# Edge-block steps of a graph layer: the bias of Q is added by VectorE as it copies Q out of PSUM

## The chip, the cores and the metric

The kernel runs on one core of one Trainium2 chip. The metric is the device time of one execution in microseconds. Five engines run programs of their own and meet at semaphores: TensorE (PE; its weight loads are listed as PEld), VectorE (DVE), ScalarE (ACT), GpSimd (POOL) and SyncE (SP), which issues most of the DMAs.

## The reference, cut to what matters

There are 50,000 nodes of 256 features and 12,500 edges. The first layer is an attention over the edges, with 8 heads of 32:

```python
qkv = x @ W_qkv.T + b_qkv
Q, K, V = ...                                   # 256 columns each
att = einsum('mhd,mhd->mh', Q[receivers], K[senders]) / sqrt(32)
attention = softmax of att over the edges that share a receiver
out = segment_sum(attention[:, :, None] * V[senders], receivers)
x = layernorm(x + out @ W_ff.T + b_ff)
```

A second layer (embeddings of the senders, filters from the edge attributes, a segment sum, one more product and a layernorm) follows. All of it is float32, and the output is 50,000 x 256.

## The kernel before, in words

Nodes without an edge need only the two layernorms and one product. So a first pass goes over all nodes as if none had an edge, and a last pass works out the rows that are receivers again and scatters them over the first result.

The first pass has 98 steps (`for g in range(G)` on every engine), each with 512 nodes: four groups of 128 rows. Nine steps in (`LEAD = 9`) the 49 edge blocks join in: step g also works on block b = g - 9, with 256 edges. These 49 steps, 9 to 57, are the edge-block steps. In a block the rows of x for the receivers (`xd`) and the senders (`xs`) were gathered by GpSimd two steps ahead. The order within a step is written out by hand, engine by engine:

- **PE**: `columns(b)` transposes xd and xs into PSUM banks A and A+1 (8 passes); `z_product(g, 0)` is the first half of the node product (12 passes, lines 845 to 847); `x_transposes(g + 1)` (8 passes, line 831); then `q_product(b)` into bank C, `k_product(b)` into bank A, `v_product(b)` into bank A+1 (14, 14 and 12 passes) and `z_product(g, 1)` (12 passes). Q and K are products in three parts (high x high, high x low, low x high), accumulated in PSUM, and each half of them starts with one pass that puts the bias row there (line 888). `q_product` waits for `xd_hi` and `xd_lo`, and `k_product` for `xs_hi` and `xs_lo`, before their first passes.
- **ScalarE**: `parts(b)` copies the transposed rows out of PSUM (`xd_hi`, `xdT`, `xs_hi`), then squares, the copy `z_hi`, a scaling (`final`), and at the end of the step `q_copy(b)` (line 1156) and `v_copy(b)` (line 1163).
- **VectorE**: `y(g - 1, 1)` (line 1442), `stats(g + 2)` (line 1414), `receiver_low(b)` (`xd_lo`, line 1468), `y(g, 0)`, `source_low(b)` (`xs_lo`, line 1473), `moments`, two small reciprocals, `z_low(g + 1)` (line 1479), `scores(b)` (lines 1487 and 1492) and its quarter of `final(g - 1)` (line 1460).
- **GpSimd**: `z_add(g + 3)` (line 682), four gathers of rows (lines 730 and 736), and one or two gathers of types (line 724), two in every other step.

`scores(b)` multiplies K, which it reads from bank A, by Q, which it reads from `qr` in SBUF, and adds up each head. `columns(b + 1)` on PE waits for that product (`e_prod`), since it writes into bank A again, and `q_product(b + 1)` waits until bank C was read (`e_q`).

Of the kernel before, what the change touches and what calls it, by code (L numbers as in the profile page):

```python
# [31 lines left out]
P = 128  # L32
ALU = mybir.AluOpType
ACT = mybir.ActivationFunctionType
# [12 lines left out]
def after(eng, sem, count):  # L47

    if count > 0:
        eng.wait_ge(sem, count)  # L50


def build(nc, x, src, dst, attr, weight, ntype, w_qkv, b_qkv, w_ff, b_ff, table, w_dist, b_dist, w_comb, b_comb, out):
    N, D = x.shape
# [34 lines left out]
    def sb(name, shape, dt=F32):  # L89
        return ctx.enter_context(nc.sbuf_tensor(name, shape, dt))  # L90

    def sem(name):
        return ctx.enter_context(nc.semaphore(name))
# [4 lines left out]
    ps = ctx.enter_context(nc.psum_tensor("ps", [P, 8, 512], F32))  # L98

    def bank(k):  # L100
        return ps[:, k, :].rearrange("p (c n) -> p c n", c=2)
# [42 lines left out]
    w_hi, w_lo = (sb(n, [P, DC, 3 * D], F32R) for n in ("w_hi", "w_lo"))  # L144
    b_raw = sb("b_raw", [P, 3, D])
    b_hi = sb("b_hi", [P, 3, D], F32R)
    b_rows = sb("b_rows", [P, 3, D], F32R)
    ones_r = sb("ones_r", [P, P], F32R)
# [82 lines left out]
    xs_hi, xs_lo, xd_hi, xd_lo = (sb(n, [P, 2, EB], F32R) for n in ("xs_hi", "xs_lo", "xd_hi", "xd_lo"))  # L231
    ze_hi, ze_lo = (z_lo[:, 0, c, :].rearrange("p (c n) -> p c n", c=2) for c in range(DC))
    xdT, vT = (sb(n, [P, 2, 2, EB]) for n in ("xdT", "vT"))
    qr, kr = (sb(n, [P, 2, EB]) for n in ("qr", "kr"))
# [84 lines left out]
    e_qp = sem("q_product")  # L319
    e_kp = sem("k_product")  # L320
    e_vp = sem("v_product")
    e_q = sem("q_copied")
    e_v = sem("v_ready")
    e_prod = sem("qk_ready")
    e_att = sem("scores_ready")
# [78 lines left out]
    def inside(g):  # L404

        return 0 <= g < G
# [9 lines left out]
    def relaxed(g):  # L416

        return g < LEAD or g >= AFTER
# [5 lines left out]
    def within(b):  # L424

        return 0 <= b < B
# [9 lines left out]
    def flat(a):  # L436
        return a.rearrange("p c n -> p (c n)")
# [6 lines left out]
    A, AB, C = 5, slice(5, 7), 7  # L444
# [373 lines left out]
    def _(pe):  # L818
        mm = pe.matmul
# [61 lines left out]
                    last = pe.transpose(bank(A + 1)[:, c, t * P:(t + 1) * P], xs[:, par, t, c * P:(c + 1) * P], ident[:])  # L881
            last.then_inc(e_xsp, 1)

        def edge_product(to, hi, lo, o):

            for t in range(2):
                e = t * P
                mm(to[:, t, :], ones_r[:], b_rows[:, o // D, :], start=True, stop=False)  # L888
                for k in range(DC):
                    mm(to[:, t, :], hi[:, k, e:e + P], w_hi[:, k, o:o + D], start=False, stop=False)  # L890
                    mm(to[:, t, :], hi[:, k, e:e + P], w_lo[:, k, o:o + D], start=False, stop=False)  # L891
                    last = mm(to[:, t, :], lo[:, k, e:e + P], w_hi[:, k, o:o + D], start=False, stop=k == DC - 1)  # L892
            return last

        def q_product(b):
            pe.wait_ge(e_xdh, b + 1)
            pe.wait_ge(e_xdl, b + 1)
            after(pe, e_q, b)
            edge_product(bank(C), xd_hi, xd_lo, 0).then_inc(e_qp, 1)

        def k_product(b):
            pe.wait_ge(e_xsh, b + 1)
            pe.wait_ge(e_xsl, b + 1)
            pe.wait_ge(e_xdc, b + 1)
            edge_product(bank(A), xs_hi, xs_lo, D).then_inc(e_kp, 1)

        def v_product(b):
            to = bank(A + 1)
# [116 lines left out]
        for g in range(G):  # L1025
            b = g - LEAD
# [59 lines left out]
    def _(act):  # L1086
        def zT_copy(g):
            for c in range(DC):
                act.wait_ge(n_tp, 2 * g + c + 1)
                after(act, n_y, 2 * (g - 1))  # L1090
                to = z_hi if in_parts(g) else zT
                act.activation(to[:, g % 2, c, :], ps[:, c, :], ACT.Identity, bias=bff_col[:, c:c + 1]).then_inc(n_tc, 1)  # L1092

        def std1(g):
            q = g % SLOTS
            np_, nj = size(g)
            act.wait_ge(n_mv, g + 1)
            after(act, n_r1, g - SLOTS + 1)
            act.activation(sd1[0:np_, q, 0:nj], mv[0:np_, q, 0:nj, 1], ACT.Sqrt, bias=eps_col[0:np_, :]).then_inc(n_s1, 1)
# [50 lines left out]
            after(act, e_vp, n)  # L1150
            act.activation(flat(xs_hi), ps[:, A + 1, :], ACT.Copy).then_inc(e_xsh, 1)

        def q_copy(b):
            act.wait_ge(e_qp, b + 1)
            after(act, e_prod, b)
            act.activation(flat(qr), ps[:, C, :], ACT.Copy).then_inc(e_q, 1)

        def v_copy(b):
            par = b % 2
            act.wait_ge(e_vp, b + 1)  # L1160
            after(act, e_vo[par], 16 * (b // 2))
            for c in range(2):
                act.activation(vT[:, par, c, :], bank(A + 1)[:, c, :], ACT.Identity, bias=bqkv[:, 4 + c:5 + c]).then_inc(e_v, 1)  # L1163
# [57 lines left out]
        for g in range(G):  # L1221
            b = g - LEAD
            if inside(g + 1):
                std1(g + 1)
            if within(b):
                parts(b)
            if inside(g - 1):
                squares(g - 1, 0)
            if relaxed(g) and inside(g + 1):
                zT_copy(g + 1)  # L1230
            if g == 4:
                act.wait_ge(s_echain, 7)
                act.activation(ct[:, 3, :], ct[:, 2, :], ACT.Sin, bias=half_pi[:], scale=-float(np.pi) / CUTOFF).then_inc(s_sin, 1)
            if inside(g - 1):
                squares(g - 1, 1)
                std2(g - 1)
            if not relaxed(g):
                zT_copy(g + 1)
            if inside(g - 2):
                final(g - 2)  # L1240
            if g == 5:
                bias_copies()
            if g == 6 or g == 7:
                weight_copies(g - 6)
            if g == 3:
                act.wait_ge(s_wready, 2)
                for k in range(DC):
                    act.activation(mix_hi[:, k, :], w_mix[:, k, :], ACT.Copy).then_inc(s_mix, 1)
            if within(b):
                q_copy(b)  # L1250
                v_copy(b)
            if g == AFTER + 13:
                act.wait_ge(c_step, step["difference"])
                act.activation(ex_c[:], run_c[:], ACT.Exp, scale=SCALE).then_inc(c_ex, 1)
            if g == AFTER + 33:
                act.wait_ge(s_tyt, 1)
                act.activation(ty_rows[:], ps[0:T, A, 0:P], ACT.Copy).then_inc(s_tyc, 1)
# [29 lines left out]
    def _(dve):  # L1287
# [193 lines left out]

        by_chunk = att[:].rearrange("p (g r h) -> p r g h", g=TL, h=H8)

        def scores(b):
            dve.wait_ge(e_kp, b + 1)
            dve.wait_ge(e_q, b + 1)
            dve.tensor_tensor(prod[:], ps[:, A, :], flat(qr), ALU.mult).then_inc(e_prod, 1)
            dve.wait_ge(e_prod, b + 1)
            heads = prod[:].rearrange("p (t h f) -> p t h f", t=2, f=HD)
            r, g = divmod(2 * b, TL)  # L1490
            if g + 1 < TL:
                dve.tensor_reduce(by_chunk[:, r, g:g + 2, :], heads, AX.X, ALU.add).then_inc(e_att, 1)
            else:
                dve.tensor_reduce(by_chunk[:, r, g, :], heads[:, 0], AX.X, ALU.add)
                dve.tensor_reduce(by_chunk[:, r + 1, 0, :], heads[:, 1], AX.X, ALU.add).then_inc(e_att, 1)
# [189 lines left out]
        for g in range(G):  # L1685
            b = g - LEAD
            if inside(g - 1):
                y(g - 1, 1)
            if inside(g - 2) and relaxed(g - 1):
                rstd2(g - 2)  # L1690
            if inside(g + 2):
                stats(g + 2)
            if within(b):
                receiver_low(b)
            y(g, 0)
            if within(b):
                source_low(b)
            if inside(g + 2):
                moments(g + 2)
            if inside(g + 1):  # L1700
                rstd1(g + 1)
            if inside(g - 1) and not relaxed(g):
                rstd2(g - 1)
            if in_parts(g + 1):
                z_low(g + 1)
            if within(b):
                scores(b)
            if inside(g - 1) and not relaxed(g):
                if relaxed(g - 1):
                    dve.wait_ge(n_od, g - 1)  # L1710
                final(g - 1)
            if g == 2:
                edge_floats()
            if g == 3:
                edge_cutoffs()
            if g == 5:
                edge_indices()
            if g == 6 or g == 7:
                weight_low(g - 6)
            if g == 7:  # L1720
                bias_parts()
            if g == 4:
                dve.wait_ge(s_mix, 2)
                for k in range(DC):
                    dve.tensor_tensor(mix_lo[:, k, :], w_mix[:, k, :], mix_hi[:, k, :], ALU.subtract).then_inc(s_mix, 1)
            if g == LEAD + 30:
                table_parts()
            softmax_step(g - AFTER)
# [44 lines left out]
```

## Time and profile before

| | |
|---|---|
| median of 3 runs | 1124.53 us (1122.92 to 1125.94) |
| profiled execution | 1127.21 us, span of its instructions 1125.5 us |
| PE busy in the span | 1058.2 us (94%) |
| VectorE busy | 918.4 us (82%) |
| ScalarE busy | 802.3 us (71%) |
| GpSimd busy | 811.4 us (72%) |
| granted TensorE clock, mean | 0.978 of full speed |
| edge-block steps | about 71 to 539 us of the span |

Busy times of the profile are sums of the durations of instructions. Matmuls are pipelined: the profile gives one of them 0.28 us while the next starts 0.12 us after it, so what a pass costs is read from the distance of two starts and not from its duration. The same holds, by less, for VectorE, where one instruction can start some hundredths before the recorded end of the one before.

### The profile page before, as it was taken

The page shows a single profiled execution, that of the slowest core. Times are in us where ns is not written, and L with a number is a line of the kernel's source. Part 1 is how long each engine was busy: PE and PEld are TensorE (multiplying, and loading weights), DVE is VectorE, ACT ScalarE, POOL GpSimd, SP SyncE. Part 2 cuts the span into 40 slices and gives each one's busy share as a digit, 9 for nine tenths or more (in the row PEclk, how much of TensorE's full clock was granted, in tenths as well). Part 3 has the DMA queues.
Part 4 walks back from the last instruction along what each step waited for, and adds up shares of the span by engine and source line. Part 5 has one row for each costly group of instructions (what it writes and reads, how often), then busy time and mean ns, then how long its engine had stood idle before and what let it go on. Part 6 is the DMA issues. An engine that isn't in the chain of part 4 may idle for free.

```text
span 1125.5 us, 25645 instructions
## 1 busy us (share of the span) xinstructions
PE 1058.2 (94%) x7302; PEld 983.2 (87%) x7302; DVE 918.4 (82%) x2643; ACT 802.3 (71%) x2452; POOL 811.4 (72%) x656
## 2 busy tenths in 40 slices
PE   5889999999999999999979799989999999999993
PEld 4679999999999999999858588879989888889882
DVE  5867888888888888888998889758888888888882
ACT  3876777777777777777767688875666666666663
POOL 5588878787888788886788888844666666666663
PEclk9999999999999999999989899989999999999997
DMA  4866666666666666665545457765666666666640
GB/s 152 305 241 215 229 228 229 224 231 221 228 217 230 208 232 216 231 219 207 190 166 200 158 206 238 276 195 164 177 174 186 188 183 186 186 189 193 186 140 33
DMA packets 121388, 227.26 MB, mean 202 GB/s; under 512 B 33588, under 2 KB 61487, under 8 KB 121185
## 3 DMA queue, kind: packets, MB, share of 16 engines
q1 hardware_dynamic: 104000, 189.54, 50.6%
q0 software_dynamic: 17248, 36.08, 11.3%
q8 instruction: 60, 0.98, 0.4%
q14 instruction: 80, 0.65, 0.2%
HBM read 137.84 MB, written 93.59 MB: 206 GB/s over the span
## 4 chain that ended last, share of the span: by engine, by line
PE 52%; DVE 26%; issue 10%; ACT 7%; SPq 2%; DVEq 1%; DMA 1%; POOL 0%; ACTq 0%; POOLq 0%
PE ps L852 7%; DVE num L1619 5%; PE ps L831 5%; PE ps L891 4%; PE ps L890 4%; PE ps L892 4%; PE ps L847 4%; PE ps L845 4%; PE ps L846 4%; DVE zeT L1630 3%; DVE est L1656 3%; DVE agg L1643 3%; PE ps L888 2%; ACT t L1196 2%; DVE msg L1639 2%
## 5 line engine op out<-in xcount | busy, mean ns | idle before, releaser
L682 POOL TENSOR_TENSOR zin<-xin,bff_row 128x1024 f32<-128x1024 f32 x98 | 233.1, 2379 | 39.3 <-DVE stat L1414 18.5
L1442 DVE SCALAR_TENSOR_TENSOR yn<-ps,r,bc 128x256 f32<-128x256 f32 x391 | 169.0, 473 | 64.0 <-PE ps L847 40.5
L852 PE MATMUL ps<-w_mix,zT 128*128 128x256 f32 x780 | 189.4, 394 | 10.1 <-ACT zT L1092 5.4
L852 PEld LDWEIGHTS ps<-w_mix,zT 128*128 128x128 f32 x780 | 147.8, 197 | 34.4 <-ACT zT L1092 10.7
L1107 ACT ACTIVATE junk<-yn 128x256 f32<-128x256 f32 x391 | 157.8, 415 | 12.3 <-DVE yn L1442 12.0
L743 POOL TENSOR_TENSOR ev<-abc,v 128x512 f32<-128x512 f32 x49 | 62.0, 1266 | 115.5 <-DVE zeT L1630 115.5
L1414 DVE BATCH_NORM_STATS2 stat<-zin 128x6 f32<-128x256 f32 x391 | 135.3, 407 | 1.9 <-issue 1.5
L724 POOL DMA_INDIRECT ty<-in_node_type_dram,src_i x98 | 103.2, 1053 | 25.7 <-issue 23.1
L730 POOL DMA_INDIRECT xd<-in_x_dram,idx x98 | 94.8, 967 | 36.1 <-PE ps L876 13.8
L755 POOL DMA_INDIRECT out_dram<-oe,idx x98 | 101.1, 1032 | 25.4 <-issue 20.2
L845 PE MATMUL ps<-mix_hi,z_hi 128*128 128x256 f32 x392 | 114.0, 291 | 2.8 <-DVE z_lo L1479 2.8
L736 POOL DMA_INDIRECT xs<-in_x_dram,idx x98 | 93.5, 954 | 29.6 <-issue 29.3
L831 PE MATMUL ps<-ident,xin 128*128 128x128 f32 (+1 forms) x782 | 103.4, 276 | 9.3 <-DMA xin<-in_x_dram 9.3
L847 PE MATMUL ps<-mix_hi,z_lo 128*128 128x256 f32 x392 | 109.9, 280 | 0.0
L846 PE MATMUL ps<-mix_lo,z_hi 128*128 128x256 f32 x392 | 109.9, 280 | 0.0
L831 PEld LDWEIGHTS ps<-ident,xin 128*128 128x128 f32 (+1 forms) x782 | 91.8, 143 | 14.7 <-issue 9.6
L1124 ACT ACTIVATE on<-yn,r 128x256 f32<-128x256 f32 (+1 forms) x229 | 101.0, 498 | 0.2 <-DVE r L1452 0.2
L973 PE MATMUL ps<-wc,agg 128*128 128x256 f32 x392 | 98.3, 379 | 0.0
L955 PE MATMUL ps<-num,wff 128*128 128x256 f32 x392 | 93.7, 382 | 0.0
L1092 ACT ACTIVATE zT<-ps,bff_col 128x512 f32<-128x512 f32 x98 | 61.8, 678 | 37.8 <-PE ps L831 37.6
L1214 ACT ACTIVATE oe<-ye,er 128x256 f32<-128x256 f32 x98 | 44.5, 501 | 61.5 <-DVE er L1679 61.5
L1163 ACT ACTIVATE vT<-ps,bqkv 128x256 f32<-128x256 f32 x98 | 41.1, 473 | 64.9 <-PE ps L914 64.9
(212 smaller groups left out, 3377.0 us busy)
## 6 DMA issues: line engine op xcount, KB each, us to landing
xin<-in_x_dram SPq DMA_DIRECT2D x97, 512.0 KB, 4.4
out_dram<-on SPq DMA_DIRECT2D x97, 512.0 KB, 2.9
xd_o<-xdT SPq DMA_DIRECT2D x49, 256.0 KB
v_o<-vT SPq DMA_DIRECT2D x49, 256.0 KB, 2.0
v<-v_o SPq DMA_DIRECT2D x49, 256.0 KB
xd<-xd_o SPq DMA_DIRECT2D x49, 256.0 KB, 4.2
abc<-a_o SPq DMA_DIRECT2D x196, 64.0 KB
sbc<-same_o SPq DMA_DIRECT2D x49, 128.0 KB, 3.8
```

Of the source, the lines that this page charges most:

```text
L682: pool.tensor_tensor(z, xx, bb, ALU.add).then_inc(n_z, 1)
L724: pool.indirect_dma_start(ty[:, t, :], None, ntype_rows, bass.IndirectOffsetOnAxis(src_i[:, t:t + 1], 0)).then_inc(n_ty, 16)
L755: pool.indirect_dma_start(out, bass.IndirectOffsetOnAxis(idx[:, n, 4 + t:5 + t], 0), oe[:, par, t, :], None, bounds_check=N - 1, oob_is_er ...
L831: last = pe.transpose(ps[:, c, j * P:j * P + np_], xin[0:np_, q, j * D + c * P:j * D + (c + 1) * P], ident[0:np_, 0:np_])
L845: mm(to, hi, mix_hi[:, k, :], start=k == 0, stop=False)
L846: mm(to, hi, mix_lo[:, k, :], start=False, stop=False)
L847: last = mm(to, lo, mix_hi[:, k, :], start=False, stop=k == DC - 1)
L852: last = mm(ps[0:np_, half(g, j), (j % 2) * D:(j % 2 + 1) * D], zT[:, g % 2, k, j * P:j * P + np_], w_mix[:, k, :], start=k == 0, stop=k = ...
L1107: last = act.activation(junk[0:np_, j, :], yn[0:np_, q, j * D:(j + 1) * D], ACT.Square, scale=float(D ** -0.5), accum_out=ss[0:np_, q, j:j ...
L1124: last = act.activation(on[0:np_, q, j * D:(j + 1) * D], yn[0:np_, q, j * D:(j + 1) * D], ACT.Copy, scale=r2[0:np_, q, j:j + 1])
L1414: last = dve.bn_stats(stat[0:np_, g % SLOTS, j, :], zin[0:np_, g % 2, j * D:(j + 1) * D])
L1442: last = dve.scalar_tensor_tensor(out=yn[0:np_, q, j * D:(j + 1) * D], in0=ps[0:np_, half(g, j), (j % 2) * D:(j % 2 + 1) * D], scalar=r1[0 ...
```

## The change

The product of Q starts without the pass that puts the bias row into PSUM (two passes fewer in each block, one for each half), so that the first pass of the product itself clears the bank. ScalarE's copy of bank C into `qr` is left out. VectorE does it in a new function `q_rows(b)`, ahead of `scores(b)`: one `tensor_tensor` over 128 x 512, which adds `b_raw[:, 0]` (the bias of Q, loaded on all partitions) to bank C and writes `qr`. K keeps its bias passes, and V its own on ScalarE.

```diff
-        def edge_product(to, hi, lo, o):
+        def edge_product(to, hi, lo, o, bias):
             for t in range(2):
                 e = t * P
-                mm(to[:, t, :], ones_r[:], b_rows[:, o // D, :], start=True, stop=False)
+                if bias:
+                    mm(to[:, t, :], ones_r[:], b_rows[:, o // D, :], start=True, stop=False)
                 for k in range(DC):
-                    mm(to[:, t, :], hi[:, k, e:e + P], w_hi[:, k, o:o + D], start=False, stop=False)
+                    mm(to[:, t, :], hi[:, k, e:e + P], w_hi[:, k, o:o + D], start=k == 0 and not bias, stop=False)
...
-            edge_product(bank(C), xd_hi, xd_lo, 0).then_inc(e_qp, 1)
+            edge_product(bank(C), xd_hi, xd_lo, 0, False).then_inc(e_qp, 1)
...
-            edge_product(bank(A), xs_hi, xs_lo, D).then_inc(e_kp, 1)
+            edge_product(bank(A), xs_hi, xs_lo, D, True).then_inc(e_kp, 1)
...
-        def q_copy(b):
-            act.wait_ge(e_qp, b + 1)
-            after(act, e_prod, b)
-            act.activation(flat(qr), ps[:, C, :], ACT.Copy).then_inc(e_q, 1)
...
             if within(b):
-                q_copy(b)
                 v_copy(b)
...
+        def q_rows(b):
+            dve.wait_ge(e_qp, b + 1)
+            after(dve, e_att, b)
+            dve.tensor_tensor(qr[:], bank(C), b_raw[:, 0:1, :].to_broadcast([P, 2, D]), ALU.add).then_inc(e_q, 1)
...
             if within(b):
+                q_rows(b)
                 scores(b)
```

## Rows read from the trace of the kernel before

**Rows 1.** Busy time by engine, from the page: busy us, share of the span, instructions.

```profile
PE 1058.2 (94%) x7302; PEld 983.2 (87%) x7302; DVE 918.4 (82%) x2643; ACT 802.3 (71%) x2452; POOL 811.4 (72%) x656
```

**Rows 2.** Windows: length, busy us (instructions) of each engine, granted clock, DMA share, GB/s.

```profile
101.00:530.00 429.00, 428.65 (x3638) 425.78 (x3636) 348.33 (x1006) 330.81 (x951) 345.66 (x292) 1.00 0.67 223
...
590.00:700.00 110.00, 99.42 (x509) 85.13 (x510) 97.89 (x312) 87.97 (x288) 91.64 (x59) 0.94 0.58 201
```

**Rows 3.** Waits from 75 to 537 us: us in total, times, longest.

```profile
PE ps L888 <- issue: 4.1, 2, 3.7
...
DVE prod L1487 <- ACT qr L1156: 42.3, 46, 2.2
DVE yn L1442 <- PE ps L847: 39.6, 46, 1.1
...
POOL xd L730 <- PE ps L876: 13.8, 23, 1.0
```

**Rows 4.** Timeline of PE: an early step and one regular step; start, duration, instruction.

```profile
86.99 0.52 PE L888 MATMUL ps<-b_rows,ones_r 128*128 128x256 f32 x1 [3.72 <-issue]
...
201.68 0.36 PE L888 MATMUL ps<-b_rows,ones_r 128*128 128x256 f32 x1
...
203.43 0.28 PE L888 MATMUL ps<-b_rows,ones_r 128*128 128x256 f32 x1
...
205.10 0.28 PE L912 MATMUL ps<-xs_hi,w_hi 128*128 128x256 f32 x1
...
207.82 0.28 PE L847 MATMUL ps<-mix_hi,z_lo 128*128 128x256 f32 x1
...
210.23 1.03 PE L831 MATMUL ps<-ident,xin 128*128 128x128 f32 x8
211.11 0.36 PE L888 MATMUL ps<-b_rows,ones_r 128*128 128x256 f32 x1
```

**Rows 5.** Timeline of VectorE, the same steps; in brackets the idle time before.

```profile
83.71 0.48 DVE L1460 TENSOR_SCALAR_CACHE_REDUCE on<-yn,r 128x256 f32<-128x256 f32 x1 [5.00 <-POOL on L721]
...
86.22 0.67 DVE L1468 TENSOR_TENSOR xd_lo<-ps,xd_hi 128x512 fp32r<-128x512 f32 x1
...
203.29 1.37 DVE L1479 SCALAR_TENSOR_TENSOR z_lo<-ps,bff_col,z_hi 128x512 fp32r<-128x512 f32 x2
205.56 0.69 DVE L1487 TENSOR_TENSOR prod<-ps,qr 128x512 f32<-128x512 f32 x1 [0.89 <-ACT qr L1156]
206.28 0.69 DVE L1492 TENSOR_REDUCE att<-prod 128x16 f32<-128x512 f32 x1
...
208.23 0.88 DVE L1442 SCALAR_TENSOR_TENSOR yn<-ps,r,bc 128x256 f32<-128x256 f32 x2 [0.87 <-PE ps L847]
...
210.34 0.67 DVE L1468 TENSOR_TENSOR xd_lo<-ps,xd_hi 128x512 fp32r<-128x512 f32 x1
...
211.71 0.68 DVE L1473 TENSOR_TENSOR xs_lo<-ps,xs_hi 128x512 fp32r<-128x512 f32 x1
```

**Rows 6.** Timeline of ScalarE, the same step.

```profile
204.87 0.58 ACT L1156 ACTIVATE qr<-ps 128x512 f32<-128x512 f32 x1
```

**Rows 7.** Timeline of GpSimd over two steps.

```profile
206.64 2.40 POOL L682 TENSOR_TENSOR zin<-xin,bff_row 128x1024 f32<-128x1024 f32 x1
209.20 0.96 POOL L730 DMA_INDIRECT xd<-in_x_dram,idx  x1 [0.16 <-issue]
...
215.20 2.42 POOL L682 TENSOR_TENSOR zin<-xin,bff_row 128x1024 f32<-128x1024 f32 x1
218.24 0.97 POOL L730 DMA_INDIRECT xd<-in_x_dram,idx  x1 [0.61 <-PE ps L876]
```

**Rows 8.** Single lines of VectorE: duration ns min/median/max, first and last start, forms.

```profile
L1487 DVE TENSOR_TENSOR prod<-ps,qr x49: 691/692/694, 77.3 to 536.2; 128x512 f32<-128x512 f32 x49
...
L1586 DVE TENSOR_TENSOR run_c<-ps,a_c x1: 1055/1055/1055, 613.1 to 613.1; 112x896 f32<-112x896 f32 x1
...
L1546 DVE TENSOR_TENSOR next_c<-dcf x1: 3194/3194/3194, 547.8 to 547.8; 112x896 f32<-112x896 f32 x1
```

## The prediction

> **What bounds the kernel now.** I read the busy times first: PE is busy for 94% of the span, VectorE for 82% [rows 1]. An average over a span says little of one stage, so the windows came next. Between 101 and 530 us, nearly all of the edge-block steps, PE is busy 428.65 of 429 us at the full clock (1.00, the 2.4 GHz level), while VectorE has 348 and ScalarE 331 us of work [rows 2]. Then the waits of this stretch: PE's only waits are two before line 888, 4.1 us together, of which 3.7 in one early step. The others wait for PE or for each other: VectorE 42.3 us in 46 steps for ScalarE's copy of Q, and 39.6 us in 46 steps for the end of the node product [rows 3]. So PE sets the pace here, by the number of its passes.
>
> The timeline of one step shows the beat: line 888 opens the product of Q at 201.68 and again at 211.11, a step of 9.43 us [rows 4]. The 14 passes of K take from 203.43 to 205.10, 1.67 us, so one pass is worth 1.67 / 14 = 0.119 us [rows 4], and not the 0.28 that the profile gives as its duration. The 14 of Q take 1.75 us (201.68 to 203.43), because the first pass behind the transposes costs 0.08 more, whatever that pass is.
>
> **PE's part.** Two passes of 0.119 us go: 0.239 us a step. They lie on the path: `q_product` waits for `xd_lo` before its first pass, bias pass or not, so these two passes fill no wait. The extra 0.08 behind the transposes passes on to line 890. In how many steps does it count? In the first one (b = 0) it does not: VectorE stands 5.00 us until 83.71 for a piece of work on GpSimd, and PE's product of Q at 86.99 stands behind that [rows 4, 5]. GpSimd was not waiting for PE then, so what PE saves before it is swallowed. The other 48 steps are left: 48 x 0.239 = 11.47 us. (The second block's Q runs partly at half clock; two passes there are worth 0.24 to 0.43 us, which changes nothing.)
>
> At one place a rule differs from the row. The rule of the Trainium skill ("TensorE: Matmul & The Clock Gate", Wait — 56ns, not 53.3ns?) is that back-to-back matmuls at full clock start N / 2.4 GHz plus some 2.5 ns apart, an estimate of 109 ns for 256 columns; the trace has 119 ns. By the rule the sum would be 10.5 us and not 11.47.
>
> **What must not be late once PE is faster.** From the last pass of the node product (207.82) to the next Q (211.11) VectorE goes through `y`, `stats` and `xd_lo`, which ends at 210.34 + 0.67 = 211.01, only 0.10 us ahead of PE [rows 4, 5]. This looks like a second bound, but the chain starts at PE's own last pass, and neither its length nor PE's 3.29 us in that stretch changes. The change shortens the other stretch, from Q's first pass to that last pass. There `k_product` needs `xs_lo`: it ends at 211.71 + 0.68 = 212.39. PE starts 0.10 us after such an end where it really waits for it (in the early step `xd_lo` ends at 86.22 + 0.67 = 86.89 and Q starts at 86.99 [rows 4, 5]), so 212.49; K's first pass is now 1.75 us behind Q's, and would be 1.51 behind it, at 212.62. That leaves 0.13 us. It is the narrowest place of the change.
>
> **VectorE's part.** `q_rows` is new: 128 x 512, one input in PSUM, one in SBUF, float32. The nearest row is `prod`, which has the same shape, the same kinds of inputs and 691 to 694 ns in 49 executions [rows 8]; `xd_lo` with 0.67 is as near [rows 5]. That the second input is the same 256 values read twice has no row; I take 0.69. The bounds: 0.58 us, what ScalarE needs for this copy [rows 6], and 1.83 us, from the dearest float32 `tensor_tensor` in the trace, with two inputs in SBUF (3194 ns for 896 elements, times 512 / 896 [rows 8]). Its cover is the time that VectorE now idles. `z_low` ends at 203.29 + 1.37 = 204.66, and `prod` starts at 205.56 after 0.89 us of waiting for `qr` [rows 5]. PE's last pass of Q starts before 203.43 and lasts 0.28 us [rows 4], so `q_rows` need not wait: it runs 204.66 to 205.35, and `prod` follows 0.72 us after its start, at 205.38 (the distance of two dependent instructions, 205.56 to 206.28 [rows 5]). K's last pass, started near 204.98 and now 0.24 earlier, is through by then. So `prod` comes 0.18 us earlier than before, while PE's end of step comes 0.24 earlier, and the idle time before `y` goes from 0.87 to 0.81 us. Cost on the path: nothing. Cover left: 0.81 us a step; without it the 0.72 us would be paid 48 times, 35 us.
>
> **ScalarE's part.** Its copy goes, 0.58 us a step [rows 6]. It ran between a scaling and the copy of V, which waits for PE's line 914 anyway. Worth nothing by itself; but `prod` no longer waits on it, which is what pays most of `q_rows`. `e_q`, for which PE's next Q waits, now comes from VectorE about a step ahead of that use: nothing.
>
> **GpSimd's part.** Nothing is added, but its room shrinks, and it is scarce. Two steps take 2 x 9.43 = 18.86 us. In one it goes on 0.16 us after `z_add`; in the other it idles 0.61 us until PE's transposes release it [rows 7], 23 times in the stage [rows 3]. So its own need is 18.86 - 0.45 = 18.41 us for two steps, 9.21 for one. PE's new step is 9.43 - 0.24 = 9.20. GpSimd falls behind by about 0.01 us a step, 0.6 us over the stage; it works one to two steps ahead of its readers (the `z_add` of 206.64 is read by the `stats` of the next step), so this does not reach PE.
>
> **Sum.** The profiled execution took 1127.21 us, with 1125.5 of span and 1.7 around it: 1127.21 - 11.47 = 1115.7. The median of the runs shown is 2.68 us below that execution, so the forecast for the median is 1124.53 - 11.47 = 1113.1, 1.0% faster. What follows the stage is released by the end of PE's last step and moves as a whole. Only the clock may move otherwise: from 590 to 700 us the granted clock averages 0.94 [rows 2], so some 13 us there run at the 1.2 GHz level, in spells whose places change when everything shifts; I allow 3 us either way.
>
> **Rivals.**
> - *GpSimd is held up by the new instruction (slower).* GpSimd has 0.22 us to spare in a step (9.43 - 9.21). If its `z_add` stood still for the 0.69 us of `q_rows` in each step, its step would be 9.90, and the kernel slower by 48 x 0.47 = 22 us: 1147. It decides from 0.22 us of holding up on (no gain left) and is over 0.3% slower from 0.3 us on. Against it: the `z_add` at 215.20 overlaps `prod` (at about 214.99, one step after 205.56), an instruction of the same kind, and takes 2.42 us; the one at 206.64 does not and takes 2.40 [rows 5, 7]. The Trainium skill ("SBUF — State Buffer", Who interferes with whom) has VectorE and GpSimd exclude each other where VectorE runs in a two-port mode or has two SBUF inputs; by that rule `q_rows`, with one input in PSUM, holds up nobody. The trace agrees, with 0.02 us. Chance 0.04.
> - *VectorE becomes the bound (slower).* With 1.83 us `q_rows` would take 1.14 more than I count, 0.33 over the cover of 0.81: a step of 9.53, 1129 us. The gain starts to shrink at 1.5 us and is gone at 1.74. For it: the 3194 ns row. Against it: with one input in PSUM, 896 elements took 1055 ns [rows 8], 0.60 for 512. Chance 0.02.
> - *K waits for `xs_lo` (no gain).* If that comes 0.13 us later than I read, K starts no earlier, and from 0.37 us on nothing is gained: 1124.5. Nothing in the change delays it. Chance 0.05, for this and any other wait of that size.
> - *A part is given back*, by the clock after the stage, or by GpSimd's narrow room: 1118 to 1121. Chance 0.04.
>
> **Numbers.** The forecast holds with 0.85. Faster: 0.85 + 0.04 = 0.89; within 0.3%, which is about what this measurement can tell from no change: 0.05; slower: 0.06. The range is 1109 to 1118: below, the 49th step, 3 us from the clock and 1 for what a median of few runs can err; above, 3 us from the clock and 2 given back. Both slower cases and the one without gain lie outside, 0.11 together.
>
> **What the profile would show.** Right: line 888 with 98 instead of 196 passes, the distance between Q products at 9.20 us, PE without waits between 100 and 520 us, the new line near 0.69 us with no idle time before it, `prod` waiting for no one, about 0.8 us of idle time before `yn`, `z_add` unchanged at 2.4 us, and GpSimd's wait for PE's line 876 gone. Wrong: idle time of PE before line 890 or 888 (late `xd_lo` or `xs_lo`), `yn` no longer waiting for PE (VectorE is the bound), or `z_add` or the gathers longer.

## The result and the profile after

The changed kernel took 1115.02 us (median of five runs, 1111.66 to 1115.82) against 1124.53 before: a ratio of 0.991 with a 95% interval of 0.989 to 0.9929, so 8.0 to 12.4 us faster. The forecast was 1113.1. The profiled execution took 1115.02 us with a span of 1113.3, 12.2 us less than the 1125.5 before. These 12.2 compare two single executions: the one before was 2.7 us above its median (1127.21 and 1124.53), the one after is the median itself.

The timeline of PE, two regular steps (line 876 is the first transpose of a step, line 891 is `w_hi` x `xd_hi`, now the first pass of Q):

```profile
204.39 0.60 PE L876 MATMUL ps<-ident,xd 128*128 128x128 f32 x4
...
207.57 0.36 PE L891 MATMUL ps<-w_hi,xd_hi 128*128 128x256 f32 x1
...
209.09 0.28 PE L889 MATMUL ps<-b_rows,ones_r 128*128 128x256 f32 x1
...
213.60 0.60 PE L876 MATMUL ps<-ident,xd 128*128 128x128 f32 x4
...
216.78 0.35 PE L891 MATMUL ps<-w_hi,xd_hi 128*128 128x256 f32 x1
```

A step is now 9.21 us (207.57 to 216.78), where it was 9.43 [rows 4]; over the stage it averages 9.19, see below. K's first pass (line 889) stands 1.52 us behind Q's, and stood 1.75 us behind it. The 0.08 behind the transposes has passed on to line 891, as its 0.36 us shows.

The timeline of VectorE in the same steps, which answers to [rows 5]:

```profile
208.17 0.68 DVE L1468 TENSOR_TENSOR xs_lo<-ps,xs_hi 128x512 fp32r<-128x512 f32 x1
...
209.18 1.38 DVE L1474 SCALAR_TENSOR_TENSOR z_lo<-ps,bff_col,z_hi 128x512 fp32r<-128x512 f32 x2
210.47 0.68 DVE L1482 TENSOR_TENSOR qr<-ps,b_raw 128x512 f32<-128x512 f32 x1
211.26 0.69 DVE L1487 TENSOR_TENSOR prod<-ps,qr 128x512 f32<-128x512 f32 x1
...
212.98 0.08 DVE L1455 DVE_READ_ACCUMULATOR on<-yn,r 128x1 f32 x1
213.90 0.88 DVE L1437 SCALAR_TENSOR_TENSOR yn<-ps,r,bc 128x256 f32<-128x256 f32 x2 [0.83 <-PE ps L847]
```

The new line 1482 starts as soon as `z_lo` lets it and takes 0.68 us; `prod` waits for nobody any more, and before `yn` there are 0.83 us of idle time.

The waits between 75 and 530 us (us in total, times, longest), which answer to [rows 3], and the new line of VectorE by itself, which answers to [rows 8]:

```profile
PE ps L891 <- issue: 4.5, 2, 3.2
...
DVE yn L1437 <- PE ps L847: 37.9, 47, 1.1
...
POOL xd L730 <- PE ps L876: 1.2, 2, 0.8
...
L1482 DVE TENSOR_TENSOR qr<-ps,b_raw x49: 670/681/690, 76.7 to 523.2; 128x512 f32<-128x512 f32 x49
```

PE has two waits here: one of 3.2 us at 86.58, in the second block, and one of 1.30 us at 365.28, which is looked at below. GpSimd waited 13.8 us for PE's line 876 before, and waits 1.2 us now. Its timeline over two steps, which answers to [rows 7]:

```profile
203.51 2.39 POOL L682 TENSOR_TENSOR zin<-xin,bff_row 128x1024 f32<-128x1024 f32 x1
206.06 0.97 POOL L730 DMA_INDIRECT xd<-in_x_dram,idx  x1 [0.16 <-issue]
...
212.08 2.40 POOL L682 TENSOR_TENSOR zin<-xin,bff_row 128x1024 f32<-128x1024 f32 x1
214.65 0.96 POOL L730 DMA_INDIRECT xd<-in_x_dram,idx  x1 [0.16 <-issue]
...
221.91 2.40 POOL L682 TENSOR_TENSOR zin<-xin,bff_row 128x1024 f32<-128x1024 f32 x1
```

Both gathers now follow `z_add` after 0.16 us; two steps take it 221.91 - 203.51 = 18.40 us, 9.20 for one: it no longer waits for PE here.

**Where the 12.2 us of the span come from.** Milestones are the first transposes (line 876) of the third block and of the last, read from PE's timeline: 94.74 and 529.17 us before, 94.08 and 518.34 after. So 0.7 us come before the third block, 10.2 us in the 46 steps between, and 1.4 us behind them. 46 steps at 0.239 would be 11.0. What is missing has one place, block step 30. At its end VectorE also splits the embedding table (a copy and a subtraction, lines 1508 and 1510), and PE feels it at its next Q: from one line 876 to the next it took 9.93 us there before, and takes 10.65 now. Instead of 0.24 less it takes 0.72 more; the other 45 steps are 10.9 us shorter together. In the timelines of VectorE and GpSimd, before:

```profile
366.15 2.41 POOL L682 TENSOR_TENSOR zin<-xin,bff_row 128x1024 f32<-128x1024 f32 x1
...
367.64 1.08 DVE L1508 CAST tab<-tab 100x256 fp32r<-100x256 f32 x1
```

and after, with PE's wait behind it:

```profile
359.45 2.41 POOL L682 TENSOR_TENSOR zin<-xin,bff_row 128x1024 f32<-128x1024 f32 x1
...
360.06 1.96 DVE L1508 CAST tab<-tab 100x256 fp32r<-100x256 f32 x1
...
365.28 0.36 PE L891 MATMUL ps<-w_hi,xd_hi 128*128 128x256 f32 x1 [1.30 <-issue]
```

The copy ends 0.16 us after GpSimd's `z_add` in both (368.72 and 368.56; 362.02 and 361.86), however early it starts. It met `z_add` 1.49 us in before and 0.61 us in now, since GpSimd no longer waits for PE and so stands elsewhere in the step. Behind the copy `xd_lo` is late (364.51 + 0.67 = 365.18), and PE's Q starts 0.10 us after that.

### The profile page after: what moved, and what is told of

Read it like the earlier page. It is cut to its first block, busy times and chain, and to the rows that moved or that the text cites. A ratio compares the mean times of both kernels' runs of the same rounds, so it can differ in the third digit from the quotient of the medians.

```text
span 1113.3 us, 25449 instructions
## 1 busy us (share of the span) xinstructions
PE 1046.2 (94%) x7204; PEld 971.6 (87%) x7204; DVE 949.6 (85%) x2692; ACT 779.0 (70%) x2403; POOL 810.9 (73%) x656
## 3 DMA queue, kind: packets, MB, share of 16 engines
q0 software_dynamic: 17248, 36.08, 10.9%
## 4 chain that ended last, share of the span: by engine, by line
PE 55%; DVE 23%; issue 9%; ACT 6%; SPq 2%; DMA 1%; DVEq 1%; POOL 0%; ACTq 0%; POOLq 0%
PE ps L852 7%; PE ps L831 5%; DVE num L1619 5%; PE ps L891 5%; PE ps L892 4%; PE ps L893 4%; PE ps L845 4%; PE ps L846 4%; PE ps L847 4%; DVE zeT L1630 3%; DVE est L1656 3%; DVE agg L1643 3%; ACT t L1192 2%; DVE msg L1639 2%; PE ps L913 2%
## 5 line engine op out<-in xcount | busy, mean ns | idle before, releaser
L852 PE MATMUL ps<-w_mix,zT 128*128 128x256 f32 x780 | 188.5, 392 | 10.2 <-ACT zT L1093 5.5
L1108 ACT ACTIVATE junk<-yn 128x256 f32<-128x256 f32 x391 | 157.9, 415 | 10.9 <-DVE yn L1437 10.8
```

Source lines behind the costliest of these rows:

```text
L852: last = mm(ps[0:np_, half(g, j), (j % 2) * D:(j % 2 + 1) * D], zT[:, g % 2, k, j * P:j * P + np_], w_mix[:, k, :], start=k == 0, stop=k = ...
L1108: last = act.activation(junk[0:np_, j, :], yn[0:np_, q, j * D:(j + 1) * D], ACT.Square, scale=float(D ** -0.5), accum_out=ss[0:np_, q, j:j ...
```

## The experiments

Times are medians, ratios are to the kernel before on the same chip, with the 95% interval. They are medians of 4 or 5 runs, of 11 for e2 and of 2 for e5. The regular step is the mean distance of line 876 from the third block to the last in one profiled execution, without block step 30 where that is longer; for e7, e8 and e10 it is taken before the waits begin.

| kernel | us | ratio | regular step, us |
|---|---|---|---|
| changed kernel | 1115.02 | 0.991 (0.989 to 0.9929) | 9.19 |
| e1, passes alone | 1114.62 | 0.9909 (0.9892 to 0.9925) | 9.19 |
| e2, move alone | 1126.14 | 1.0007 (0.9997 to 1.0017) | 9.43 |
| e3, one more, PSUM input | 1117.11 | 0.9928 (0.9912 to 0.9944) | 9.19 |
| e4, two more, PSUM input | 1131.05 | 1.0057 (1.0039 to 1.0074) | 9.49 |
| e5, one more, SBUF inputs | 1151.9 | 1.0233 (1.0211 to 1.0256) | 9.20 and 10.70 in turn |
| e6, table later | 1113.71 | 0.9896 (0.9878 to 0.9913) | 9.19 |
| e7, no bias of K | 1106.63 | 0.9833 (0.9818 to 0.9848) | 8.96, then waits |
| e8, e7 and table later | 1106.56 | 0.9832 (0.9817 to 0.9847) | 8.96, then waits |
| e9, scaling first | 1108.45 | 0.9852 (0.9838 to 0.9865) | 9.18 |
| e10, e8 and scaling first | 1106.59 | 0.9837 (0.9823 to 0.985) | 8.95, then waits |
| e11, e10 and gathers later | 1099.28 | 0.9769 (0.9753 to 0.9785) | 8.96 |

### e1 and e2: the two halves of the change

e1, against the kernel before:

```diff
-            edge_product(bank(C), xd_hi, xd_lo, 0).then_inc(e_qp, 1)
+            edge_product(bank(C), xd_hi, xd_lo, 0, False).then_inc(e_qp, 1)   # q_copy on ScalarE stays
```

> The kernel before, with the two bias passes of Q left out on PE and nothing else changed: ScalarE still copies Q, so Q lacks its bias. Theory (PE's number of passes sets the pace, the copy's place does not matter): the distance of two steps falls from 9.43 to 9.20 us, VectorE's idle time before yn shrinks from 0.87 to about 0.63, and the time is that of the changed kernel, 1113 to 1116 us. Rival (freeing ScalarE, or ending VectorE's wait for ScalarE's copy, brought part of the gain): a step stays above 9.25 and the time above 1117.

e2, against the changed kernel:

```diff
-            edge_product(bank(C), xd_hi, xd_lo, 0, False).then_inc(e_qp, 1)
+            edge_product(bank(C), xd_hi, xd_lo, 0, True).then_inc(e_qp, 1)
```

> The changed kernel with the two bias passes put back on PE, so that the bias of Q is added twice; VectorE takes Q out of PSUM. Theory: the move costs and brings nothing, 9.43 us a step, VectorE idle about 1.05 us before yn, 1124 to 1126 us. Rival (the move brings part of the gain): under 1121. Rival (the new VectorE instruction costs something on the path, which the passes pay back): over 1127.

Two lines of VectorE's timeline in e1, and two in e2:

```profile
210.73 0.69 DVE L1488 TENSOR_TENSOR prod<-ps,qr 128x512 f32<-128x512 f32 x1 [0.89 <-ACT qr L1157]
...
213.17 0.88 DVE L1443 SCALAR_TENSOR_TENSOR yn<-ps,r,bc 128x256 f32<-128x256 f32 x2 [0.64 <-PE ps L847]
```

```profile
203.96 0.69 DVE L1482 TENSOR_TENSOR qr<-ps,b_raw 128x512 f32<-128x512 f32 x1
...
207.62 0.88 DVE L1437 SCALAR_TENSOR_TENSOR yn<-ps,r,bc 128x256 f32<-128x256 f32 x2 [1.05 <-PE ps L847]
```

Both came out as the theory has it, down to the idle times before `yn`: 0.64 and 1.05 us, where 0.63 and 1.05 were expected. The passes alone give the whole gain, with VectorE's wait for ScalarE still there. The move alone gives nothing and costs nothing. What the move is for, then, is that Q still gets its bias.

### e3 and e4: how much cover VectorE has left

```diff
+        def again(b):
+            for i in range(1):          # e4: range(2)
+                last = dve.tensor_tensor(rest[:, ...], bank(C), b_raw[:, 0:1, :].to_broadcast([P, 2, D]), ALU.add)
+            last.then_inc(e_qx, 1)      # PE's next Q waits for e_qx in the place of e_q
...
+            if within(b):
+                again(b)                # behind final(g - 1)
```

> The changed kernel with one more instruction of the form of q_rows (PSUM and SBUF input, 128 x 512), behind VectorE's part of final, where it now idles 0.79 to 0.83 us before yn; its result is read by nobody. Theory (cover of 0.8 us): it takes 0.6 to 0.7 us of that idle time and the regular step stays 9.20; the one step in which VectorE also splits the table gets longer by up to 0.7 us. 1114 to 1117 us. Rival (VectorE is already as good as the bound): each step longer by up to 0.6 us, up to 29 us more.

> As the run with one more, with two of these instructions. Theory: 1.2 to 1.35 us against 0.8 us of cover, so 0.4 to 0.55 us over; the step becomes 9.6 to 9.75 us, yn no longer waits for PE, PE idles before line 891, and the time is 1135 to 1142 us. Rival (the idle time is not real cover, since other waits take its place): the second instruction costs no more than the first.

VectorE in e3, and then VectorE and PE in e4:

```profile
212.25 0.68 DVE L1487 TENSOR_TENSOR rest<-ps,b_raw 128x512 f32<-128x512 f32 x1
213.16 0.88 DVE L1438 SCALAR_TENSOR_TENSOR yn<-ps,r,bc 128x256 f32<-128x256 f32 x2 [0.22 <-PE ps L848]
```

```profile
207.75 1.28 DVE L1487 TENSOR_TENSOR rest<-ps,b_raw 128x512 f32<-128x512 f32 x2
208.95 0.87 DVE L1438 SCALAR_TENSOR_TENSOR yn<-ps,r,bc 128x256 f32<-128x256 f32 x2
...
211.82 0.35 PE L892 MATMUL ps<-w_hi,xd_hi 128*128 128x256 f32 x1 [0.16 <-issue]
```

One more instruction is free in the regular step: 9.19 us, with 0.22 of idle time left. Two are not: `yn` follows at once, PE waits before Q (0.16 us in this row), and a step takes 9.49. So the cover is real and ends where it was said to end. The size was less than I expected: 1131 us, not 1135 to 1142. I had added durations. Instructions that don't depend on each other start 0.60 us apart here (two of them and then `yn`: 208.95 - 207.75 = 1.20), and in the changed kernel `yn` starts 0.92 us after the instruction before it (212.98 to 213.90), of which the view shows 0.83 as idle. 1.20 - 0.92 = 0.28 us over, and 9.19 + 0.28 = 9.47.

e3 as a whole is 2 us slower than the changed kernel, and its step 30 is the place: 13.29 us in the profiled execution, which at 1118.22 us was the longest of the four. The table's copy starts at 359.94, lasts 2.52 us, and PE then waits 2.47 us before Q. Its passes behind that wait, and the windows there:

```profile
365.98 0.42 PE L893 MATMUL ps<-w_lo,xd_hi 128*128 128x256 f32 x1
366.19 0.41 PE L894 MATMUL ps<-w_hi,xd_lo 128*128 128x256 f32 x1
...
365.70:369.00 3.30, 3.29 (x16) 3.30 (x17) 3.30 (x12) 1.68 (x4) 2.39 (x4) 0.51 0.58 211
```

They start 0.21 us apart with a granted clock of 0.51, the 1.2 GHz level, until 369.18. 16 passes at 0.21 and not 0.12 are 1.5 us on top of the wait. So a wait of PE can be paid a second time, in the clock. It need not be: earlier in the same execution PE waited for longer, and its passes behind that start 0.12 us apart, with a granted clock of 1.00 from 85 to 90 us:

```profile
87.47 0.36 PE L892 MATMUL ps<-w_hi,xd_hi 128*128 128x256 f32 x1 [3.41 <-DVE xd_lo L1464]
87.66 0.28 PE L893 MATMUL ps<-w_lo,xd_hi 128*128 128x256 f32 x1
87.78 0.28 PE L894 MATMUL ps<-w_hi,xd_lo 128*128 128x256 f32 x1
```

This early wait stands in every kernel up to e8. Behind it the clock stayed at the full level in e3 (3.41 us), e6 (2.80) and e7 (3.04), and fell to the 1.2 GHz level in the changed kernel (3.15), e1 (2.83) and e2 (2.62). What decides it is not shown.

### e5: the same instruction with both inputs in SBUF

```diff
-                last = dve.tensor_tensor(rest[:, ...], bank(C), b_raw[:, 0:1, :].to_broadcast([P, 2, D]), ALU.add)
+                last = dve.tensor_tensor(rest[:, ...], b_raw[:, 1:2, :].to_broadcast([P, 2, D]), b_raw[:, 0:1, :].to_broadcast([P, 2, D]), ALU.add)
```

> As the run with one more VectorE instruction of 128 x 512 in each step, at the same place, but with two inputs in SBUF instead of one in PSUM and one in SBUF. It falls where GpSimd's z_add is under way. Theory (only an instruction with two SBUF inputs gets in GpSimd's way): VectorE stands until z_add ends, the instruction takes up to 2 us instead of 0.7, a step becomes 10 us or more and the time 1140 to 1180 us. Rival (no such conflict, the long durations after 540 us had another cause): the same time as with the PSUM input, 1114 to 1117 us. The Trainium skill (SBUF — State Buffer, Who interferes with whom) states the first.

The line by itself in e3 and in e5 (duration ns min/median/max), and two steps of VectorE and GpSimd in e5:

```profile
L1487 DVE TENSOR_TENSOR rest<-ps,b_raw x49: 682/685/690, 84.0 to 528.8; 128x512 f32<-128x512 f32 x49
```

```profile
L1487 DVE TENSOR_TENSOR rest<-b_raw x49: 683/690/2809, 83.2 to 562.0; 128x512 f32<-128x512 f32 x49
...
204.99 0.68 DVE L1487 TENSOR_TENSOR rest<-b_raw 128x512 f32<-128x512 f32 x1
...
214.19 2.51 DVE L1487 TENSOR_TENSOR rest<-b_raw 128x512 f32<-128x512 f32 x1
216.63 0.86 DVE L1438 SCALAR_TENSOR_TENSOR yn<-ps,r,bc 128x256 f32<-128x256 f32 x2
...
202.68 2.40 POOL L683 TENSOR_TENSOR zin<-xin,bff_row 128x1024 f32<-128x1024 f32 x1
...
213.73 2.41 POOL L683 TENSOR_TENSOR zin<-xin,bff_row 128x1024 f32<-128x1024 f32 x1
```

The two kernels differ in where one input lies, and by 35 us. At 204.99 GpSimd only has the last 0.09 us of its `z_add` to do, and the instruction takes 0.68. At 214.19 it starts 0.46 us into a `z_add`, and ends at 216.70, 0.56 us after that ends (216.14). These steps take 10.7 us, the others 9.20. So the price in the second rival of the prediction, 1.83 us, was too low (2.51 measured here, 2.81 at most). It had been scaled by the number of elements, and that is not what sets it: in all 24 long executions of e5 the instruction ends 0.56 us after the `z_add` that it met, so what it costs is mostly what is left of that `z_add`. The trace before had this already, in a subtraction with two SBUF inputs that met a `z_add` in the first of its two executions and none in the second:

```profile
L1725 DVE TENSOR_TENSOR mix_lo<-w_mix,mix_hi x2: 410/1080/1750, 46.6 to 48.3; 128x256 fp32r<-128x256 f32 x2
```

The condition under which this is paid is two inputs in SBUF. `q_rows` does not meet it: 670 to 690 ns in all 49 executions. That alone would prove little, since it runs beside a `z_add` in only one of the 49, for 0.15 us. The proof is e3: there the instruction of the same form runs beside a `z_add` for at least 0.3 us in 27 of 49 steps, takes 0.68 to 0.69 us in each, and `z_add` takes 2.39 to 2.43 us as before. The Trainium skill ("SBUF — State Buffer", Who interferes with whom) says this of two SBUF inputs beside a GpSimd instruction that reads SBUF, and the trace agrees; it calls the conflict an exclusive lock, and here VectorE waited until the `z_add` had ended.

### e6: the table's split moved

```diff
-            if g == LEAD + 30:
-                table_parts()
+            if g == AFTER + 30 or g == AFTER + 32:
+                table_parts((g - AFTER - 30) // 2)     # the copy, then the subtraction
```

> The changed kernel with VectorE's two instructions that split the embedding table (lines 1508 and 1510) taken out of block step 30 and put, one each, into steps 88 and 90, where only the node product runs. Theory (there the cover of VectorE is used up, and a two-SBUF-port copy waits for z_add, which made this one step 10.65 us): the step falls to 9.20, 1.4 us less in the stage, and 0 to 0.7 us come back in the late steps: 1113 to 1114.5 us. Rival (that step is long for another reason): still 10.6 us.

The long step is gone: no step from the third block on differs from 9.19 by 0.15 us, and the 46 steps take 422.9 us and not 424.3. The copy now takes 0.26 us; so 0.26 is its own duration, and the rest of the 1.08 and 1.96 was waiting. The late step is no safe place by itself: in e8, with the same edit, the copy met a `z_add` there, took 2.42 us and ended 0.16 us after it. The time is 1.3 us below the changed kernel's with overlapping intervals, so the step shows the gain and the time of the whole kernel alone would not.

### e7, e8 and e10: what bounds next

```diff
-            edge_product(bank(A), xs_hi, xs_lo, D, True).then_inc(e_kp, 1)
+            edge_product(bank(A), xs_hi, xs_lo, D, False).then_inc(e_kp, 1)
```

> The changed kernel with K's two bias passes left out as well, nothing put in their place. The scores of all edges of one receiver then differ by the same number, Q times the bias of K, which the softmax over these edges cancels. Theory A (PE alone sets the pace): 8.96 us a step, 11.5 us less, 1103.5. Theory B (GpSimd needs 9.21 us a step; PE runs ahead of it until the lead of 7 to 9 us is used up, after 28 to 38 steps): 8.96 us at first, 9.21 at the end, 1105 to 1108 us. Rival (GpSimd binds at once): no gain, 1115.

> Both: K's bias passes left out and the split of the table moved to steps 88 and 90. Theory: what the two bring adds up, about 1 to 1.6 us below the run without K's bias alone, unless GpSimd is by then the bound, in which case the long step only lets it catch up and the move brings less than 0.5 us.

e10 adds, on GpSimd:

```diff
+            if g == LEAD:
+                final(g - 2)                # ahead of the gathers of step 9
             if within(b) and within(b + 2):
                 receivers(b + 2)
                 senders(b + 2)
...
-            if inside(g - 2) and relaxed(g - 1):
+            if inside(g - 2) and relaxed(g - 1) and g != LEAD:
```

> K's bias passes left out and the split of the table moved, as before, and GpSimd's scaling put first. Theory (without K's bias passes GpSimd is the bound by the end of the stage): PE starts 4 us earlier and only uses up GpSimd's lead sooner, so that the end stays where it was, 1105 to 1107 us, with the waits for the gathers beginning ten to fifteen steps earlier. Rival (PE still sets the pace, the waits for gathers are incidental): 1102 to 1103 us.

PE's waits in e7 (75 to 530 us), and the first of them in its timeline:

```profile
PE ps L876 <- DMA xs<-in_x_dram,idx: 4.6, 6, 1.7
...
290.06 0.66 PE L876 MATMUL ps<-ident,xd 128*128 128x128 f32 x4 [0.70 <-DMA xs<-in_x_dram,idx]
```

K's bias cancels in the softmax, so its two passes can go as well. PE then makes 8.96 us a step, but only up to block 23; from 290 us on it waits again and again for gathered rows. The gain was 8.4 us of the 11.5 that PE alone would give: theory B, with GpSimd's need of 9.2 us a step. Its lead ran out five steps before the range of 28 to 38. Part of that is one pause of GpSimd, 1.15 us at 253.42, where 0.16 is the rule: 1.0 us of lead, or four steps at 0.25 us. The gathers have to land too, which I had counted loosely: the last one for the wait at 290.06 was issued by 285.18, 4.9 us before. In e8 the first wait comes in step 31. That is not the work of its edit, which changes nothing before step 30: in its profiled execution the third block starts 1.2 us later than in e7 (93.28 and 92.04), so the same need of GpSimd is felt later. In e10 PE starts 2.9 us earlier than in e8 (90.43), and the first wait comes in step 17. The three end alike: 1106.63, 1106.56 and 1106.59 us. A saving on PE, on VectorE or at the start that leaves the total where it was is the mark of another engine's bound, here GpSimd's.

### e9: the wait at the start

The edit of e10 on GpSimd, on the changed kernel alone.

> The changed kernel, with GpSimd's last scaling before the stage (line 721, for step 7) put ahead of the gathers of step 9 and not behind them. In the run of the changed kernel VectorE stands 4.4 us for it and PE 3.2 us before the second product of Q. Theory (that wait swallowed what the first block saves, and PE paces the rest, with GpSimd 7 to 9 us ahead): the wait goes, the whole stage starts some 4 us earlier and ends so, 1110.5 to 1112 us. Rival (GpSimd paces the stage, since it needs 9.21 us a step and PE 9.19): no gain, 1114 to 1116.

VectorE's instruction that waited 4.4 us for GpSimd in the changed kernel now goes at once:

```profile
78.91 0.47 DVE L1457 TENSOR_SCALAR_CACHE_REDUCE on<-yn,r 128x256 f32<-128x256 f32 x1
...
80.52 0.88 DVE L1439 SCALAR_TENSOR_TENSOR yn<-ps,r,bc 128x256 f32<-128x256 f32 x2 [1.13 <-PE ps L849]
```

The third block's transposes start at 89.40 and not at 94.08, 4.7 us earlier: 3.15 us of PE's wait, and some 1.5 us since no passes at half clock follow it. The stage keeps that. The second part is luck of the execution compared, since e6 has the wait without the half clock, and its third block starts at 91.92. The result, 1108.45 us, is below my range of 1110.5 to 1112. Most of what is left is step 30 once more: the stage was 2.0 us shorter, and the table's copy took 288 ns here, since it fell into a gap of `z_add`. As in e1 to e3 (1.85, 1.27 and 2.52 us), its length depends on where GpSimd stands at that moment.

### e11: a version that beats both

```diff
+    LATE = [AFTER + k for k in (8, 9, 10, 17, 18, 19, 25)]
...
-                if b % 2 == 1:
+                if b % 2 == 1 and b // 2 >= len(LATE):
                     type_gather(B + b // 2)
+            if g in LATE:
+                type_gather(B + LATE.index(g))
```

> As the run before, and seven of the 24 second type gathers of the stage (those of blocks 1, 3, ... 13) are issued in seven late steps in which GpSimd idled 0.6 to 2.3 us. Theory (GpSimd is the bound; 7 x 1.26 = 8.8 us taken from it): PE keeps 8.96 us a step through the stage and waits for no gather, and the time falls to 1097 to 1100 us. Rival (the transfers themselves are late, not their issue): the waits for gathers stay and the time is that of the run before.

The windows of e11 (columns as in [rows 2]):

```profile
92.00:260.00 168.00, 168.00 (x1428) 166.86 (x1427) 154.60 (x436) 127.54 (x372) 139.86 (x118) 1.00 0.72 239
260.00:500.00 240.00, 239.61 (x2033) 237.79 (x2033) 221.07 (x620) 182.71 (x537) 199.63 (x170) 1.00 0.72 234
```

Seven of GpSimd's gathers less in the stage and PE is busy 239.61 of 240 us again, with 8.96 us a step until the last blocks and 0.7 us of waits for gathers in all. 1099.28 us is 2.3% below the kernel before and 7.3 us below e10, which differs in these seven gathers alone. Leaving them out of the stage takes away their transfers as well as their issuing, but the trace tells the two apart. In e10, from step 18 to step 36, GpSimd is done issuing a block's last gather only 3.0 to 4.9 us before its transposes; in e11 it is 6.8 to 11.8 us before them.

## Why the prediction was right, and where it was off

- **PE sets the pace, and each step gets two passes shorter.** Right, and shown: 0.239 us a step forecast, 9.434 - 9.189 = 0.245 measured between e2 and e1, and e1 alone gives the whole gain. The cheaper pass by the rule in the Trainium skill ("TensorE: Matmul & The Clock Gate", Wait — 56ns, not 53.3ns?), an estimate of 109 ns and so of 0.218 us a step, fits less well.
- **`q_rows` costs 0.69 us of VectorE and nothing on the path.** Right: 0.68 us, and e2 shows no cost (1.0007). It started 0.09 us earlier than I reckoned, since it need not wait for the recorded end of `z_low`, and `prod` follows 0.79 us behind its start and not 0.72, so 0.83 us of idle time are left and not 0.81.
- **The first block counts for nothing.** Right as to the wait, which e9 takes away. But the start of the stage wanders by more than the term: the third block begins anywhere between 91.9 (e6) and 94.7 us (e4, before) with the same program on GpSimd (e5, at 96.9, left out). The changed kernel and e6 are the same program up to there, and lie 2.2 us apart, 1.5 of them from Q's start on (86.58 to 94.08, and 85.93 to 91.92): passes at half clock in one execution and not in the other. So the 0.7 us that came from there are not shown to be an effect of the change.
- **`k_product` and `xs_lo`, 0.13 us apart.** They did not collide: `xs_lo` ends at 208.85, K starts at 209.09, and no wait of PE is listed there.
- **GpSimd needs 9.21 us a step and is not reached.** Right in both halves: 9.20 us without waiting for PE, and e7, e8 and e10 show what happens when PE goes below it. I had priced this narrow room only for a GpSimd that is held up, not as the limit of the next saving.
- **The sum.** 11.47 us were forecast, 9.5 measured (8.0 to 12.4), 12.2 in the profiled executions. The measured interval holds the forecast. The mechanism was right; a term was missing from the sum. "The other 48 steps are left" took all of them to be alike, and block step 30 is not: it costs 1.5 us over a regular step (10.65 - 9.19) where it cost 0.5 before (9.93 - 9.43), because its copy waits longer for GpSimd's `z_add`. So 1.0 us is given back there, and PE's wait of 1.30 us before line 891 in that step is the one sign of being wrong that the prediction named and the profile shows. Moving the copy (e6) makes the 46 steps 1.3 us shorter. The rest of the difference between 9.5 and 11.5 is inside the interval and has no cause shown; the medians of the kernel before alone ran from 1124.53 to 1126.0 in the four sets of runs. What follows the last block's transposes took 596.4 us before and 594.5 to 596.3 in the changed kernel and in e1 to e6, so the 3 us allowed either way for the clock were too many.
- **The rivals.** VectorE as the bound needs 0.92 us more in a step than `q_rows` takes (e3, e4), or two SBUF inputs beside `z_add` (e5). That GpSimd is held up was not seen: in the steps shown `z_add` takes 2.39 to 2.40 us, and in e3, where VectorE's instruction often runs beside it, 2.39 to 2.43. K waiting for `xs_lo` did not happen.

## What to carry to other kernels

Where one engine is busy without a pause, count its instructions by the distance of their starts, and work moved off it is worth that distance for as long as the engine that takes it has idle time before its next wait for the first. Work out for every other engine what it needs in a step, also for those that lose nothing: the one with the least room is the next bound, and here it took back a quarter of the next saving (3.1 of 11.5 us). Look for the step in the loop that is unlike the others, since the room used up is missing there first.

## What the runs showed of the hardware

- A VectorE instruction of 128 x 512 with one input in PSUM took 0.68 to 0.69 us beside GpSimd's `z_add` (27 steps of e3), and up to 2.81 us with both inputs in SBUF (e5). A float32 copy of 100 x 256 from SBUF to SBUF took 0.26 us alone and 1.08, 1.96 and 2.52 us when it started inside a `z_add`; it ended 0.16 us after that each time.
- After a wait of 2.47 us, PE ran at the 1.2 GHz level for its next 16 passes (granted clock 0.51), which cost another 1.5 us (e3). After the 1.30 us wait in the changed kernel it did not, nor after waits of 3.41 us (e3), 3.04 (e7) and 2.80 (e6): the length of the wait does not decide it alone.
- Independent VectorE instructions of 0.68 us start 0.60 us apart; where one waits for the other's semaphore, the next starts after 0.72 to 0.79 us (0.72 from `prod` to `att`, 211.26 - 210.47 = 0.79 from `q_rows` to `prod`).
